# A graph network layer with residual and layer norm: the node rows of the first seven quads are made in the setup, whose work is laid out in 32 units

## The reference, cut to what matters

```
s, v = x[:, :64], x[:, 64:].reshape(n, 32, 3)
h_s, h_v = s @ lin1_ws * a / 8, einsum(v, lin1_wv) * a / sqrt(32)
w = silu(edge_attr_64 @ fc_w1 / 8) @ fc_w2 / 8               # 224 weights per edge
es, ev = h_s[src], h_v[src]                                  # the gather
m  = products of w, es, ev and edge_attr_4                   # 96 scalars, 128 vectors
agg = segment_sum(m, dst) / 4
pre = (self connection of x) * a + (agg @ lin2) * a
x = layernorm(x + [silu(pre scalars), sigmoid(gates) * pre vectors])
```

## Time and profile before

| | us |
|---|---|
| median of 3 runs | 4014.98 (4014.16 to 4015.4) |
| span of the profiled execution | 4805.3 |
| PE busy | 3953.4 (82%) |
| POOL busy | 2967.8 (62%) |
| VectorE busy | 2421.9 (50%) |
| ScalarE busy | 1987.8 (41%) |
| edge block begins in the profile | 74.1 |
| last gather begins in the profile | 4767.4 |

### The profile page before, as it was taken

The page is one execution under the profiler, slowest core; times in us unless marked ns, Lnnn a source line. Parts: engine busy times, 40 slices in busy tenths (PEclk is TensorE's granted clock), DMA queues, the critical chain, the costliest instruction groups (busy, mean ns, idle before and its releaser), DMA issues.

```text
span 4805.3 us, 64016 instructions
## 1 busy us (share of the span) xinstructions
PE 3953.4 (82%) x18658; PEld 1603.5 (33%) x18658; DVE 2421.9 (50%) x7622; ACT 1987.8 (41%) x5178; POOL 2967.8 (62%) x3160
## 2 busy tenths in 40 slices
PE   8778888888888888888888888888888888888887
PEld 5233333333333333333333333333333333333333
DVE  5455545555454544555555445555545545454544
ACT  3344444444444444344444344444444434444444
POOL 3666666666666666666666666666666666666664
PEclk9999999999999999999999989999999999999999
DMA  6443434343434343334343334343434333333333
GB/s 216 146 106 102 106 102 106 102 107 102 108 99 108 102 106 97 105 102 106 103 107 101 104 99 105 102 106 103 107 103 106 102 105 103 105 103 104 103 103 87
DMA packets 366207, 515.47 MB, mean 107 GB/s; under 512 B 66498, under 2 KB 245578, under 8 KB 365486
## 3 DMA queue, kind: packets, MB, share of 16 engines
q0 software_dynamic: 150768, 256.60, 22.7%
q10 hardware_dynamic: 164378, 180.74, 12.1%
q1 hardware_dynamic: 50724, 74.13, 5.1%
HBM read 431.15 MB, written 80.06 MB: 106 GB/s over the span
## 4 chain that ended last, share of the span: by engine, by line
another core or an unknown queue 35%; ACT 21%; PE 20%; issue 14%; ACTq 8%; SPq 0%; DMA 0%; DVE 0%; DVEq 0%
ACT aggsb L759 13%; ACTq L778 6%; PE pst_e L1061 6%; PE psg L1074 5%; PE psg L1072 5%; ACT tsum L783 3%; PE psw L1053 3%; ACTq L766 2%; ACT L804 1%; ACT hid L749 1%; PE psx L1097 1%; PE psx L1045 1%; ACT vec_s L800 0%; ACT L749 0%
## 5 line engine op out<-in xcount | busy, mean ns | idle before, releaser
L710 POOL DMA_INDIRECT rows<-h_table,src_cols x3125 | 2953.5, 945 | 1799.9 <-issue 894.8
L557 DVE TENSOR_TENSOR prod<-psw,rows 128x384 f32<-128x384 f32 (+2 forms) x3128 | 1210.1, 449 | 1680.8 <-remote 1264.3
L1072 PE MATMUL psg<-tsum,shifts 128*64 128x320 f32 x3126 | 1101.8, 478 | 653.3 <-ACT tsum L783 462.6
L1053 PE MATMUL psw<-fc,hid 128*128 128x448 f32 x3128 | 1424.0, 579 | 7.7 <-issue 1.7
L759 ACT ACTIVATE aggsb<-psg 32x160 f32<-32x160 f32 x3128 | 917.0, 293 | 927.2 <-remote 744.2
L1074 PE MATMUL psg<-tsum,shifts 128*64 128x288 f32 x3126 | 1009.2, 449 | 0.0
L1053 PEld LDWEIGHTS psw<-fc,hid 128*128 128x128 f32 x3128 | 549.0, 196 | 949.6 <-issue 840.1
L1061 PE MATMUL pst_e<-prod,sel 128*32 128x448 f32 x6256 | 811.9, 593 | 2.4 <-issue 2.4
L1072 PEld LDWEIGHTS psg<-tsum,shifts 128*64 128x64 f32 x3126 | 385.9, 144 | 1122.2 <-ACT tsum L783 774.3
L783 ACT ACTIVATE tsum<-pst_e 128x448 f32<-128x448 f32 x782 | 424.8, 543 | 499.0 <-remote 369.4
L1045 PE MATMUL psx<-es,fc 128*128 128x512 f32 x782 | 415.7, 613 | 175.5 <-ACT turned L788 120.5
(11 more groups left out here) (151 smaller groups left out, 1511.2 us busy)
## 6 DMA issues: line engine op xcount, KB each, us to landing
es<-in_esP ACTq DMA_DIRECT2D x391, 256.0 KB
agg_table<-aggsb ACTq DMA_DIRECT2D x782, 80.0 KB
rows<-h_table,src_cols POOLq DMA_INDIRECT x3125
nag<-agg_table SPq DMA_DIRECT2D x96, 320.0 KB
nxin<-in_xN SPq DMA_DIRECT2D x96, 208.0 KB
h_table<-hrow ACTq DMA_DIRECT2D x24, 320.0 KB, 4.2
out<-yn SPq DMA_DIRECT2D x95, 80.0 KB
xa<-in_xaT SPq DMA_DIRECT2D x24, 256.0 KB, 4.0
```

The lines of the kernel that those rows point to most:

```text
L557: return nc.vector.tensor_tensor(out, w_part, ev, ALU.mult)
L710: nc.gpsimd.indirect_dma_start(out=rows[:, u * QT + j, :], out_offset=None, in_=m.h, in_offset=bass.IndirectOffsetOnAxis(ap=m.src[:, t:t + ...
L1053: ins = nc.tensor.matmul(psw[b][:, 2 * c:2 * c + 2, 0:WN], hid[:, at:at + P], m.fc2[:].rearrange("p (t w) -> p t w", t=2)[:, :, 0:WN], sta ...
L1072: nc.tensor.matmul(psg[0:2 * W, 0:2 * AW].rearrange("p (s c) -> p s c", s=2), shifts[:, q % PRING, h, 0:2, :], low, start=(h == 0), stop=( ...
```

## The change

- **Rows made in the setup.** The input `xg` holds x row by row in the order of the kernel, with a as column 161. POOL gathers in the setup the x rows of tiles 0 to 27 (seven quads) by src into the memory of `prod`. For each of these quads TensorE turns four blocks of 128 columns and one of the joined last 32 columns (`turn`), ScalarE and VectorE copy them out, and the same lin1 products as for a chunk follow; the result times a goes straight into slots 0 to 6 of `rows`. The edge block's gathers begin at quad 7, and its products wait for no gather in the first seven quads.
- **Units.** The setup is a list of 32 units, written out: 25 chunks (h) and 7 quads (x), the x units after chunks 9, 11, 14, 16, 18, 21 and 23. A quad is turned two units ahead and its copy made one ahead. The warm product stays in the first six units only.
- **Copying out.** Three of four blocks go through two banks to ScalarE, the fourth and the last axis of all four through three banks to VectorE.
- **Tests.** `dst` is loaded in two halves, and `dst_in_window` and its extremes are made in quarters between the units. Window offsets come from new loads of each quad's four window starts (`quad_base`) in contiguous columns; the test of all dst against the next quad's start is one of window starts. `window_base` is copied by POOL, the loads of the fc weights go to SP's queue. `tile_offset` is kept as two rows per partition.
- **Waits.** SP doesn't wait for the stores of `h_table`; POOL does, ahead of quad 7, and ScalarE ahead of the first late load of `e4`, whose memory now holds the setup's buffers. POOL's waits in the edge block follow `freed(q)`: up to quad 15 a slot's own last user, up to quad 47 by pairs quad q - 7, from 48 on quad q - 3 as before.

```
-CHECKS = 9
+CHECKS = 15
...
+LOOSE = 6 * RING
...
+AHEAD = RING - 1
+XBEFORE = [9, 11, 14, 16, 18, 21, 23]
+WARM_UNITS = 6
+UNITS = [unit for c in range(HCHUNKS + 1) for unit in [("h", c)] + [("x", j) for j in range(AHEAD) if XBEFORE[j] == c]]
...
+        later = m.e4[:, E4_FIRST:TILES, :].rearrange("p t k -> p (t k)")
+        at_xz, at_hrow = SLOTS * CB * P, SLOTS * CB * P + SLOTS * P
+        assert at_hrow + SLOTS * CB * F <= (TILES - E4_FIRST) * K4
+        xa = later[:, 0:at_xz].rearrange("p (s n) -> p s n", s=SLOTS)
+        xz = later[:, at_xz:at_hrow].rearrange("p (s n) -> p s n", s=SLOTS)
+        hrow = later[:, at_hrow:at_hrow + SLOTS * CB * F].rearrange("p (s b f) -> p s b f", s=SLOTS, f=F)
...
+        flat = m.prod[:].rearrange("p r t w -> p (r t w)")
+        xg = flat[:, 0:AHEAD * QT * XW].rearrange("p (t f) -> p t f", f=XW)
+        xt = sb("x_turned", [P, CB * P])
+        xzt = sb("x_last_turned", [P, P])
+        xlast = sb("x_last", [P, P])
...
-        psh = [ctx.enter_context(nc.psum_tensor(f"psh{i}", [P, 2, 512], F32)) for i in range(2)]
-        psp = ctx.enter_context(nc.psum_tensor("psp", [P, 512], F32))
+        psl = [ctx.enter_context(nc.psum_tensor(f"psl{i}", [P, 512], F32)) for i in range(2)]
+        psr = [ctx.enter_context(nc.psum_tensor(f"psr{i}", [P, 512], F32)) for i in range(3)]
         psf = ctx.enter_context(nc.psum_tensor("psf", [P, 512], F32))
+        pxt = ctx.enter_context(nc.psum_tensor("pxt", [P, 512], F32))
+        pxz = ctx.enter_context(nc.psum_tensor("pxz", [P, 512], F32))
+        psp = pxz[:, P:P + 2]
...
+            def load_x(c, width):
+                if c >= SLOTS:
+                    sp.wait_ge(s_high, unit_of("h", c - SLOTS) + 1)
+                    sp.sem_inc(s_tick, 1)
+                sp.dma_start(xa[:, c % SLOTS, 0:width], io["xaT"][:, c * CB * P:c * CB * P + width]).then_inc(s_xin[c % SLOTS], 16)
+                sp.dma_start(xz[:, c % SLOTS, :], io["xzT"][:, c * P:c * P + P]).then_inc(s_xin[c % SLOTS], 16)
...
+            load_x(HCHUNKS, rest)
             sp.dma_start(m.e4[:, 0:E4_FIRST, :], io["e4T"][:, 0:E4_FIRST, :]).then_inc(s_edge, 16)
-            sp.dma_start(m.src[:, 0:SRC_FIRST], io["srcT"][:, 0:SRC_FIRST]).then_inc(s_edge, 16)
-            for c in range(SLOTS):
-                sp.wait_ge(s_hout[c], 16 * (rounds + (2 if c == 0 else 0)))
-            sp.wait_ge(s_edge, 32)
+            sp.wait_ge(s_fc, 1)
+            sp.sem_inc(s_tick, 1)
+            for dst, src in late:
+                sp.dma_start(dst, src).then_inc(s_fcw, 16)
+            sp.wait_ge(s_edge, 16)
+            sp.wait_ge(s_fcw, n_fcw)
...
-            for dst, src in late:
-                pool.dma_start(dst, src).then_inc(s_w, 16)
-            pool.wait_ge(s_w, n_w)
+            pool.wait_ge(s_src, 16)
+            for t in range(AHEAD * QT):
+                nc.gpsimd.indirect_dma_start(
+                    out=xg[:, t, :], out_offset=None, in_=io["xg"],
+                    in_offset=bass.IndirectOffsetOnAxis(ap=m.src[:, t:t + 1], axis=0)).then_inc(s_xrow[t // QT], 16)
+            for half in range(2):
+                pool.wait_ge(s_dst[half], 32)
+            nc.gpsimd.tensor_copy(m.base[:], m.dst[0:1, 0:TILES:QT])
...
+            def high_part(n, kind, c):
+                blocks = 2 if (kind, c) == ("h", HCHUNKS) else CB
+                if kind == "h" and c >= SLOTS:
+                    dve.wait_ge(s_hout[c % SLOTS], 16 * (c // SLOTS))
+                    dve.sem_inc(s_tick, 1)
+                dve.wait_ge(s_high, n + 1)
+                if kind == "x":
+                    out, scale = m.rows[:, QT * c:QT * c + QT, :], xg[:, QT * c:QT * c + QT, F:XW]
+                elif c < HCHUNKS:
+                    out, scale = hrow[:, c % SLOTS, :, :], a_rows[:, CB * c:CB * c + CB].unsqueeze(2)
+                else:
+                    out, scale = hrow[:, c % SLOTS, 0:blocks, :], m.a[:, done:done + blocks].unsqueeze(2)
+                if blocks == CB:
+                    nc.vector.tensor_scalar(out[:, CB - 1, 0:P], psr[n % 3][:, P:2 * P], scale[:, CB - 1, :], None, ALU.mult)
+                nc.vector.tensor_tensor(out[:, :, P:F], psr[n % 3][:, 0:V * blocks].rearrange("p (b c) -> p b c", c=V),
+                                        scale.to_broadcast([P, blocks, V]), ALU.mult).then_inc(s_highcp, 1)
...
+            def quarter(k):
+                return slice(TILES // 4 * k, TILES // 4 * k + TILES // 4)
+            def local_nodes(k):
+                dve.wait_ge(s_dst[k // 2], 32)
+                then(nc.vector.tensor_tensor(m.local[:, quarter(k)], m.dst[:, quarter(k)], tbase[:, quarter(k)], ALU.subtract))
+            def extreme(n, of, op):
+                return nc.vector.tensor_reduce(ext[:, n:n + 1], of, AX.X, op)
+            def window_starts():
+                dve.wait_ge(s_bases, 16 * (QT + 1))
+                nc.vector.tensor_tensor(m.off[:, 0, :], qbase[:], qfirst[:], ALU.subtract)
...
+            for n, (kind, c) in enumerate(UNITS):
+                if x_unit(n + 3):
+                    j = UNITS[n + 3][1]
+                    dve.wait_ge(s_xrow[j], 16 * QT)
+                    nc.vector.tensor_copy(xlast[:].rearrange("p (t c) -> p t c", c=V),
+                                          xg[:, QT * j:QT * j + QT, P:F]).then_inc(s_xlast, 1)
+                if x_unit(n + 1):
+                    dve.wait_ge(s_xps, UNITS[n + 1][1] + 1)
+                    nc.vector.tensor_copy(xzt[:], pxz[:, 0:P]).then_inc(s_xzcp, 1)
+                if n == 0:
+                    dve.wait_ge(s_a, 32)
+                high_part(n, kind, c)
...
+                for k in range(4):
+                    if k and n == 8 + 3 * k:
+                        local_nodes(k)
+                    if n == 9 + 3 * k:
+                        extreme(2 * k, m.local[:, quarter(k)], ALU.max)
+                    if n == 10 + 3 * k:
+                        extreme(2 * k + 1, m.local[:, quarter(k)], ALU.min)
...
+            def turn(j):
+                pe.wait_ge(s_xrow[j], 16 * QT)
+                for t in range(QT):
+                    nc.tensor.matmul(pxt[:, P * t:P * t + P], xg[:, QT * j + t, 0:P], m.ident[:], start=True, stop=True,
+                                     is_transpose=True, skip_group_check=True)
+                pe.wait_ge(s_xlast, j + 1)
+                nc.tensor.matmul(pxz[:, 0:P], xlast[:], m.ident[:], start=True, stop=True,
+                                 is_transpose=True, skip_group_check=True).then_inc(s_xps, 1)
+            for n, (kind, c) in enumerate(UNITS):
+                if x_unit(n + 2):
+                    if UNITS[n + 2][1] == 0:
+                        pe.wait_ge(s_ident, 1)
+                    turn(UNITS[n + 2][1])
+                if kind == "h":
+                    if n < WARM_UNITS:
+                        keep_warm(256)
+                    pe.wait_ge(s_xin[c % SLOTS], 32 * (c // SLOTS + 1))
+                    left, last = xa[:, c % SLOTS, :], xz[:, c % SLOTS, :]
+                else:
+                    pe.wait_ge(s_xcp, c + 1)
+                    pe.wait_ge(s_xzcp, c + 1)
+                    left, last = xt[:], xzt[:]
+                if n >= 2:
+                    pe.wait_ge(s_lowcp, n - 1)
+                blocks = 2 if (kind, c) == ("h", HCHUNKS) else CB
+                for b in range(min(blocks, CB - 1)):
+                    ins = rows_of(n, b, LASTN if blocks == 2 and b == 1 else P, left)
+                ins.then_inc(s_low, 1)
+                if n >= 3:
+                    pe.wait_ge(s_highcp, n - 2)
+                if blocks == CB:
+                    rows_of(n, CB - 1, P, left)
+                last_axis(n, blocks, last).then_inc(s_high, 1)
...
+            def low_half(n, kind, c):
+                if kind == "h" and c >= SLOTS:
+                    act.wait_ge(s_hout[c % SLOTS], 16 * (c // SLOTS))
+                    act.sem_inc(s_tick, 1)
+                act.wait_ge(s_low, n + 1)
+                for b in range(2 if (kind, c) == ("h", HCHUNKS) else CB - 1):
+                    width = LASTN if (kind, c) == ("h", HCHUNKS) and b == 1 else P
+                    r = slice(0, width)
+                    if kind == "x":
+                        out, scale = m.rows[:, QT * c + b, 0:P], xg[:, QT * c + b, F:XW]
+                    else:
+                        out = hrow[r, c % SLOTS, b, 0:P]
+                        scale = a_rows[:, CB * c + b:CB * c + b + 1] if c < HCHUNKS else m.a[r, done + b:done + b + 1]
+                    ins = nc.scalar.activation(out, psl[n % 2][r, P * b:P * b + P], ACT.Copy, scale=scale)
+                ins.then_inc(s_lowcp, 1)
...
+            for c in range(len(m.h_stored)):
+                pool.wait_ge(m.h_stored[c], m.h_stores[c])
+                pool.sem_inc(stores_seen, 1)
...
+            def freed(q):
+                if q < 2 * RING:
+                    return max(0, q - RING + 1)
+                if q % GROUP:
+                    return 0
```

(9 more changed lines are left out.)

356 lines of the change are left out of this document (194 added, 162 removed).

## The result

The changed kernel takes 3994.71 us (median of 4 runs, 3993.66 to 3996.47), the kernel before beside it on the same chip 4015.06 (4014.16 to 4015.4): ratio 0.995, interval 0.9937 to 0.9962, a gain of 20.3 us. The forecast was 3987 and a gain of 28. The time lies in the range of 3979 to 4005, but not in the forecast's own 3982 to 3993: it is 0.3 us short of where rival 1 (a slower start) begins.

The account below looks back on a forecast made before the run. POOL's gathers were taken as the bound, 5.003 us a quad against TensorE's 4.66. Quad 48 begun at 285.5 instead of 314.9 gave 29.4, taken as 28: 4015 - 28 = 3987 us; forecast 3982 to 3993, range 3979 to 4005.

Parts of the forecast that it names:

- rival 1: Setup: start slower than its rows say (PE clock, or transfers ending at 75); gain 10 to 20, 3995 to 4005; chance 0.22.
- POOL as the bound: Edge loop: POOL's gathers set the timed runs' end, 5.003 us a quad against TensorE's 4.66.
- 4805 - 786: Profile before: span 4805.3 less 786 us of true waiting on POOL gives 4019 us, within 4 us of the timed median.
- 28 gathers less: POOL in the edge loop: 28 x 1.2508 = 35.0 us saved, of which 29.4 kept; 28 taken.
- The loop to quad 48: Edge loop: quad 45 summed at 282.4, plus 3 us of handovers, so quad 48 gathered at 285.5 instead of 314.9.
- The rival's 212 us at clock 0.95: Edge loop: TensorE runs the 45 quads at clock 0.95, 201 us become 212, gain 18; no chance of its own.
- The setup: Before the edge loop: PE's units sum to 57.8 us, ending at 67.2; edge loop starts at about 72 instead of 74.1.
- C: Experiments' theory on the setup: starved TensorE makes it long; for late_shift, edge loop at 70 to 74, 3985 to 3988 us.
- E: Experiments' rival for late_shift: transfers bound the setup whatever the order; edge loop at 77 or later, 3991 us or more.
- 2: Edge loop: TensorE and ScalarE's loop, not POOL, bounds at 5.0 us; gain only 4 us, 4011; chance 0.10.
- 3: Edge loop: POOL never stands at quad 48 since the loop has caught up; time 3980; chance 0.05.
- 4: Setup: VectorE holds up the x gathers and they the setup; start 109, time 4023 at 3.1 us a gather; chance 0.05.

Follow-up runs that it names:

- extra28: Changed kernel with 28 more gathers, one after every 27th quad, into memory nobody reads: 4027.64 us.
- late_loads: Changed kernel with the loads for the tests issued after chunks 11, 15 and 19 instead of 5, 7 and 9: 3991.67 us.
- late_shift: Changed kernel with test loads after chunks 8, 13 and 17 and VectorE's test passes four units later: 3993.48 us.
- h_only: Changed kernel without the x units and their 28 setup gathers, 25 chunks only, all quads gathered in the edge block: 4013.8 us.
- warm_all: Changed kernel with the warm product in all 25 chunks; it overwrote the miss count and took the slow general path: 58869 us.
- late_loose: late_loads with the looser rule for gathers kept up to quad 96 (`LOOSE = 12 * RING`): 3986.81 us.

## Why the prediction was right, and where not

**POOL as the bound**: right, shown by extra28 (32.9 us for 28 gathers), by the table's constant rest, and by the second trace of the kernel before, which the 4805 - 786 had reconstructed to 6 us. What I made of those halts was wrong: I took them for the profiler's, and said they would return. No later profile had them.

**28 gathers less**: 35 us forecast; 3906.6 - 3874.6 = 32.0 measured, after 3.4 us of stand at quad 8 (forecast 1.5) and 1.2 at quad 48 (forecast 4.2, from 281.3 to 285.5). At quad 8, the first sums ended at 93.5, 9.8 us after the first product, and I had 9.2; POOL was ready 6.7 us after that product (89.09 and a gather), not 7.7, since the first gather came 1.6 us after the edge loop's start and not 2.7. At quad 48 POOL stood less for two reasons, both counted from the edge loop's start at 83.5: TensorE was 2.0 us quicker than forecast (211.5 for 213.5), and POOL, which had stood longer at quad 8, was ready 1.0 us later (210.3 for 209.3).

**The loop to quad 48**: the prediction has 213.5 us from the edge loop's start (72 to 285.5), the trace 211.5 (83.5 to 295.0). With rows of 4.25, 4.36 and 4.66 us a quad and 3 us of handovers, that is right to 2 us, and the clock, 0.83 from 80 to 100 us, did no more harm than the start of before had done in the earlier trace rows. The rival's 212 us at clock 0.95 for the 45 quads fell: 93.5 to 295.0 is 201.5.

**The setup is the step that failed**: "That ends when PE does, so I add 2 us for units that find no data", and with it "the edge loop starts at about 72 us". It started at 83.5, and those 11.5 us, less the 2 of the loop, are the 9.5 us by which quad 48 was late (295.0 for 285.5). That is more than the 7.7 us from 3987 to 3994.7, because the forecast had already taken 28 for a sum of 29.4. The last product of the setup ended at 80.75 instead of 67.2, 13.5 us later. The sum by the trace:
- a unit is quicker than forecast: 1.12 us (57.11 to 58.23), not 1.54, since the ten matmuls of one chunk follow each other at 0.11 us each, where the forecast took 0.13 to 0.16 for each of eight and 0.18 for the two of the last axis from the earlier trace rows. 31 units by 0.42: 13.0 less.
- waits for chunks, 11.9 us in three waits, and 5.8 us for copies of turned axes, 17.7 more; 2 were forecast.
- products at 1.2 GHz after those waits, 24.8 to 46.2 and 73.8 to 77 us: some 1.2 us a unit and 0.55 a turn, 8.8 more.

-13.0 + 17.7 + 8.8 = 13.5, if the 2 us of the forecast stay out of both sides (67.2 had them not). That the time still lies in the range is in part luck: the loss by waits and clock, 26.5 us, was halved by units that were mis-sized the other way. The forecast of the transfers was good, 69.3 us of all engines against 68.2 in the windows up to 80; the error was to compare sums, PE 57.8 and transfers 65.4, and to see them end together. Transfers that are full from 10 us on give a chunk when they have it; what the queue puts before a chunk, 3.1 MB for the tests ahead of chunk 8 and 3.9 MB ahead of chunk 10, stops TensorE, and what it loses then (and its clock) isn't given back. The kernel before had the same share of 1.06 and no wait. Two things differ, and no run takes them apart: its PE needed 2.44 us a chunk where a unit now takes 1.12, and its loads for the tests stood behind chunk 7 (11.94 us in its second trace) and not behind 5. The second average was VectorE's: "about 49 us in 60: beside PE". 48.9 are in the windows, but 2.3 and 3.3 of them in the starved tens and 9.4 and 9.7 from 50 to 70. There each x unit waits 0.64 to 0.67 us for a copy behind a test pass, once 2.08.

How these shares part is not settled. Moving loads relieved the chunks and hit a copy (late_loads), moving the tests too hit the chunks again (late_shift); h_only, without x units, kept 12.2 us. The full share of the transfers up to 50 us and more is in all of them, and no order that was tried got the start below 76.9 with the x units in; that they bound the first half is argued from this, since the kernel that would part C from E was not run. That the fallen clock costs the 8.8 us is read from the products' times; the one run meant to test the clock, warm_all, failed. That VectorE bounds the second half is read from the windows and was not tried by itself.

**Rivals.** 1 was the nearest: its mechanism named transfers "that end at 75"; they ended before that, and its other half, the clock, came in the setup. 2 fell with extra28. 3 (POOL never stands at quad 48) is not so, by 1.2 us; made true by hand, it is worth just these. 4 fell for this kernel: the 28 gathers in the setup are at 942 to 1058 ns (source view of L304), and end at 44 us, as forecast.

```profile
L304 POOL DMA_INDIRECT prod<-in_xg,src_cols x28: 942/946/1058, 9.1 to 43.1; - x28
```

But its mechanism is real. In late_loose, which has the same gathers with VectorE's work shifted against them, two of 28 are long (timeline of POOL and VectorE):

```profile
32.52 0.97 DVE L402 TENSOR_TENSOR dst_in_window<-dst_cols,tbase 128x782 f32<-128x782 int32 x1 [4.63 <-DMA tbase<-in_tile_base]
32.98 1.33 POOL L304 DMA_INDIRECT prod<-in_xg,src_cols  x1 [0.30 <-issue]
...
39.53 0.96 DVE L402 TENSOR_TENSOR dst_in_window<-dst_cols,tbase 128x782 f32<-128x782 int32 x1
39.61 1.70 POOL L304 DMA_INDIRECT prod<-in_xg,src_cols  x1 [0.30 <-issue]
...
41.19 0.96 DVE L405 TENSOR_REDUCE ext<-dst_in_window 128x1 f32<-128x782 f32 x1
41.61 0.94 POOL L304 DMA_INDIRECT prod<-in_xg,src_cols  x1 [0.30 <-issue]
```

Both end 0.82 us after a difference on L402 ends (33.49 to 34.31, 40.49 to 41.31), as do the longest of the changed kernel (1.06 us, 41.98 to 42.80) and of late_shift (1.59 us, 41.25 to 42.07). In the ten traces that have these gathers, 12 began under an L402, and all 12 end 0.81 to 0.83 us after it, whatever was left of it when they began. A gather that began 0.06 us ahead of one (40.85 us in late_loads) took its usual 0.95 us. None of those that began under a reduction of the same length is stretched by it: they took 0.94 to 0.98 us (0.94 at 41.61). Three that began under the copies of 0.2 us took 0.94 to 0.98, but behind so short an operation a wait of this kind could not be seen. So the int32 difference, which has two operands in SBUF, holds up a gather that begins under it until it is over. The Trainium skill, SBUF — State Buffer, "SBUF: two separate sides", describes such a lock, with descriptor writing blocked until VectorE is done, and here the traces agree in kind; its 3100 ns, that the prediction's 4041 us came from, have 1.70 us as their largest counterpart. In late_loose it cost POOL 0.4 and 0.75 us, in the changed kernel 0.1, in a time in which POOL has 40 us to spare.

**A better kernel**: late_loose, two constants and three numbers away, 3986.81 us, 0.9932 of before (0.9918 to 0.9946), where the changed kernel has 0.995.

## What to carry to other kernels

When two resources are each nearly full in a stage, don't compare their sums: lay the transfers out in the order of their queue and ask for each unit when its data lands, since a consumer that became quicker is one that waits for loads; loads that nobody needs yet belong behind those that someone does, and a pass that waits for such a load must not stand ahead of a copy that the critical engine needs. Count the instructions of the engine that sets the end (here 1.25 us for each of GpSimd's gathers, to within 2 us in 35), then look for the rule that hands the gain back: each wait on slots at the point where the saving is to be spent. And take one odd profile of a kernel for one execution until a second has been seen.
